# An audio tower with 64 experts: waits in place of a memset ahead of each indirect transfer

## The chip, the cores and the metric

The kernel runs on one core of a Trainium2 chip. The metric is the time of one execution on the device in microseconds (us). A core has five engines that work side by side, each with an instruction queue of its own: PE (TensorE, matmuls), DVE (VectorE), ACT (ScalarE), POOL (GpSimd) and SP (SyncE, which here only issues transfers). They are held together by semaphores: an instruction may wait for one to reach a count, and raise one when it is done.

## The reference

The input x is 128 series of 125 positions with 64 channels, float32. The convolution has a stride of two, so 128 x 63 = 8064 tokens are left. Three stages follow one another: the convolution with a norm over time and channels and a PReLU, a selective scan over 64 channels x 16 states, and a layer of 64 experts of which each token uses two. The change touches the third.

```python
    h = _L0_tok_ref(x, L0_tok_w, L0_tok_b, L0_tok_gamma, L0_tok_beta, L0_tok_alpha)
    h = h + _L0_attn_ref(_layernorm(h, axis=-1), L0_attn_A_log, L0_attn_D_param, L0_attn_scale, L0_attn_W_dt, L0_attn_b_dt, L0_attn_W_B, L0_attn_b_B, L0_attn_W_C, L0_attn_b_C)
    h = h + _L0_ffn_ref(_layernorm(h, axis=-1), L0_ffn_Wr, L0_ffn_br, L0_ffn_W1, L0_ffn_b1, L0_ffn_W2, L0_ffn_b2)
```

and the third of them:

```python
        logits = xf @ Wr + br
        topk_logits, topk_idx = jax.lax.top_k(logits, TOP_K)
        gates = jax.nn.softmax(topk_logits, axis=1)
        combine = jnp.zeros((T, E), xf.dtype).at[jnp.arange(T)[:, None], topk_idx].add(gates)
        out = jnp.zeros((T, W2.shape[-1]), xf.dtype)
        for e in range(E):
            h = jax.nn.relu(xf @ W1[e] + b1[e])
            y = h @ W2[e] + b2[e]
            out = out + combine[:, e:e + 1] * y
```

The kernel doesn't run all 64 experts over all tokens. It sorts the tokens by expert, runs each expert over its own rows, and takes the two results of a token back.

## The kernel before

All tokens lie on 128 partitions x L = 63 positions. After the convolution and the scan (the first 390 us or so) comes the expert layer, in these parts:

**Routing.** The positions are cut into three shares, SHARES = (0 to 16), (16 to 40), (40 to 63), and into eight groups of 8 positions (QG = 8): groups 0 and 1 are share 0, groups 2 to 4 share 1, groups 5 to 7 share 2. For each group PE transposes the normalised rows (transposes_of, L760) and makes the logits, ACT copies them out of PSUM (nT_copy, L1099), DVE finds the two best experts (choose) and writes a 0/1 table of them (L1503, which raises s_hot by one for each group). PE counts the tokens of each expert with matmuls on that table (counts_of, L775), DVE and ACT take the counts out (offsets_of, L1509), and DVE turns them into slot_i, for each token and choice the row of a sorted table in DRAM (slots_of, L1544, raising s_slot). DVE and PE do the routing of all three shares before they start on the experts.

**Scatter.** POOL writes each token's normalised row (64 floats) to its slot in sorted_rows[h], with an indirect transfer for each position and choice: 128 rows a transfer, 126 transfers in all (send, L613), share after share. Each raises s_disp[h].

**Experts.** They run in 80 steps: 24 for share 0, 28 for share 1, 28 for share 2. A step takes up to two pairs of tiles of 128 rows. Per step: PE transposes the rows (rows_T, L870); ACT copies them (xT_copy, L1151); PE makes the hidden layer (hidden, L881); ACT takes one half of the relu (relu_A, L1160) and DVE the other (relu_B, L1593); PE makes the outputs (outputs, L894, which waits for the y_copy of the step before); DVE copies them out of PSUM (y_copy, L1603, raising s_yb by one for each step); ACT stores them to expert_out[h] (store, which raises s_st). ACT starts a share's steps when all of that share's scatters have landed (s_disp[h]). SP loads the weights into a ring of 23 pairs and waits for s_yb before it writes over one.

**Gather.** POOL waits until all stores of a share are done (s_st, 4 semaphores) and then fetches each token's two result rows from expert_out[h] with indirect transfers into y1 and y2: 126 transfers in all (L634), 32, 48 and 46 for the shares. Each raises s_yl.

**Combine.** After the 80 steps DVE works through a block that builds the combine table (L1620, L1627), adds the bias product that PE makes of it, and then, group by group, multiplies y1 and y2 by the gates (gate_rows, L1635) and adds them to hg (L1637), waiting for s_yl; SP stores each finished group to out.

Ahead of each of POOL's 252 indirect transfers stands a memset: 128 x 128 zeros into a tile `beat` that nothing reads. It goes through ch.link, which makes the next instruction of POOL wait until the memset has ended (it raises POOL's own semaphore s_pool, and the transfer waits for it). All of this is code in a fixed order on each engine's queue; no scheduler moves it.

```python
                        ch.link(pool.memset(beat[:, :], 0.0))
                        pool.indirect_dma_start(
                            out=sorted_rows[h], out_offset=bass.IndirectOffsetOnAxis(ap=slot_i[:, c, l:l + 1], axis=0),
                            in_=xn[:, l, :], in_offset=None).then_inc(s_disp[h], 16)
```

In what follows transfers are counted d = 0 to 251 in the order of POOL's queue: d0 to 31, 32 to 79 and 80 to 125 are the scatters of the three shares, d126 to 157, 158 to 205 and 206 to 251 the gathers.

## Time and profile before

| | us |
|---|---|
| median of 3 runs (lowest, highest) | 925.29 (922.06 to 929.41) |
| the profiled execution: its time | 921.33 |
| its span, first to last instruction | 919.6 |
| PE busy | 555.3 (60%) |
| DVE busy | 568.8 (62%) |
| ACT busy | 332.5 (36%) |
| POOL busy | 654.9 (71%) |
| mean granted TensorE clock | 0.772 of full speed |

The profiled execution took 921.33 us, of which 1.7 us lie outside its span. All rows that follow are of this one execution; times in them count from the start of the span. "Idle before" is how long an engine stood still ahead of an instruction, with what ended it: another engine's line, a transfer, "issue" (nothing that the profile shows), or "remote" (the semaphore moved without an instruction in the profile that moved it at that time).

### The profile page before, as it was taken

The numbers are of one execution on the slowest core, as the hardware profiler recorded it, in microseconds if no ns is written. First come the engines' busy times: TensorE is split into PE (matmuls) and PEld (weight loads), VectorE is DVE, ScalarE is ACT, GpSimd is POOL, SyncE is SP. The second block draws the span as 40 slices with busy tenths as digits, with TensorE's granted clock in tenths as the row PEclk, the third lists the DMA queues.
The fourth block names the chain that finished last, engine by engine and source line by source line (L and its number), as shares of the span: only waits on it lengthen the run. The fifth ranks groups of instructions, "written<-read, shape, count | busy, mean of one in ns | idle before, by whom it ended". The sixth has DMA issues, their size and how long they took to land.

```text
span 919.6 us, 9334 instructions
## 1 busy us (share of the span) xinstructions
PE 555.3 (60%) x2514; PEld 372.0 (40%) x2520; DVE 568.8 (62%) x1180; ACT 332.5 (36%) x622; POOL 654.9 (71%) x645
## 2 busy tenths in 40 slices
PE   4653347575674575768556756577679765794230
PEld 4642012122221221244324545565568554683230
DVE  1697899999999999876464511132234211247964
ACT  2169756466466554342132111122224211241010
POOL 5894699999999999706848888763740387503884
PEclk9967576898798887775767667798799875797565
DMA  7999900000000000002600344467578844651012
GB/s 238 384 156 116 44 0 0 0 0 0 0 0 0 1 0 0 0 1 75 162 14 26 112 137 131 129 171 206 151 207 227 240 133 119 173 151 43 22 56 70
DMA packets 106607, 84.98 MB, mean 92 GB/s; under 512 B 30464, under 2 KB 90240, under 8 KB 106560
## 3 DMA queue, kind: packets, MB, share of 16 engines
q1 hardware_dynamic: 79312, 54.76, 27.4%
q10 hardware_dynamic: 19184, 21.40, 7.4%
q0 software_dynamic: 8064, 8.27, 3.4%
q8 instruction: 19, 0.31, 0.1%
q14 instruction: 28, 0.23, 0.1%
HBM read 57.22 MB, written 33.49 MB: 99 GB/s over the span
## 4 chain that ended last, share of the span: by engine, by line
PE 32%; POOL 30%; issue 16%; DVE 10%; another core or an unknown queue 4%; ACT 4%; SPq 1%; DMA 1%; POOLq 0%; ACTq 0%; DVEq 0%
PE ps L894 15%; POOL x_w L570 12%; POOL w_ring L563 11%; PE ps L881 6%; POOL xt L634 5%; PE ps L870 2%; PE ps L659 2%; PE ps L723 1%; PE ps L750 1%; POOL beat L633 1%; PE ps L808 1%; PE ps L745 1%; DVE lstat L1280 1%; DVE mi L1498 1%
## 5 line engine op out<-in xcount | busy, mean ns | idle before, releaser
L723 PE MATMUL ps<-x_w,ident 128*128 128x512 f32 x252 | 154.3, 771 | 102.0 <-POOL x_w L570 102.0
L563 POOL TENSOR_TENSOR w_ring<-xt,bc 128x2016 f32<-128x2016 f32 x32 | 144.7, 4524 | 13.4 <-DVE hh_ring L1409 7.3
L634 POOL DMA_INDIRECT xt<-expert_out,slot_i x126 | 123.6, 981 | 37.0 <-issue 21.9
L613 POOL DMA_INDIRECT sorted_rows<-xp,slot_i x126 | 123.0, 976 | 35.9 <-issue 18.4
L1409 DVE TENSOR_TENSOR_SCAN hh_ring<-ps,w_ring 128x1024 f32<-128x1024 f32 x64 | 145.7, 2277 | 0.1
L570 POOL TENSOR_TENSOR x_w<-hh_ring,bc 128x2016 f32<-128x2016 f32 (+1 forms) x32 | 142.4, 4456 | 2.3 <-PE ps L723 2.3
L723 PEld LDWEIGHTS ps<-x_w,ident 128*128 128x128 f32 x252 | 60.0, 249 | 199.0 <-POOL x_w L570 125.7
L633 POOL MEMSET beat<- 128x128 f32 x126 | 27.5, 218 | 106.3 <-DMA expert_out<-x_w 106.1
L1603 DVE COPY x_w<-ps 128x256 f32<-128x256 f32 x80 | 33.9, 424 | 109.2 <-PE ps L894 58.8
L1060 ACT ACTIVATE ps<-dt_t,a_exp 128x1024 f32<-128x1024 f32 x64 | 71.5, 1117 | 63.7 <-DVE hh_ring L1409 63.6
L1054 ACT ACTIVATE ps<-dt_t,a_exp 128x1024 f32<-128x1024 f32 x64 | 71.5, 1118 | 51.9 <-DVE w_ring L1388 51.9
L894 PE MATMUL ps<-dt_t,x_w 128*128 128x192 f32 x280 | 66.8, 389 | 30.6 <-issue 23.1
L1151 ACT ACTIVATE x_w<-ps 128x256 f32<-128x256 f32 x80 | 30.7, 384 | 149.3 <-PE ps L870 60.5
L1388 DVE TENSOR_TENSOR w_ring<-ps,w_ring 128x1008 f32<-128x1008 f32 x64 | 76.7, 1198 | 3.4 <-ACT ps L1054 3.4
L1403 DVE SCALAR_TENSOR_TENSOR w_ring<-ps,w_ring 128x1008 f32<-128x1008 f32 x64 | 75.5, 1180 | 0.0
L894 PEld LDWEIGHTS ps<-dt_t,x_w 128*128 128x128 f32 x280 | 54.5, 224 | 36.5 <-issue 34.1
L894 PE MATMUL ps<-x_w 128*128 128x192 f32 x224 | 53.1, 386 | 17.4 <-issue 16.7
L1593 DVE TENSOR_SCALAR x_w<-ps,dt_t 128x128 f32<-128x128 f32 x70 | 21.5, 345 | 54.0 <-remote 30.9
L894 PEld LDWEIGHTS ps<-x_w 128*128 128x128 f32 x224 | 43.5, 223 | 21.8 <-issue 19.9
L612 POOL MEMSET beat<- 128x128 f32 x126 | 27.5, 219 | 31.6 <-DVE slot_i L1544 31.5
L894 PE MATMUL ps<-bc,x_w 128*128 128x192 f32 x136 | 33.0, 391 | 25.6 <-issue 24.1
L870 PE MATMUL ps<-ident,x_w 128*128 128x128 f32 x160 | 37.3, 326 | 11.4 <-DMA x_w<-sorted_rows 11.1
(211 smaller groups left out, 956.1 us busy)
## 6 DMA issues: line engine op xcount, KB each, us to landing
dt_t<-packed SPq DMA_DIRECT2D x140, 96.5 KB
x_w<-packed SPq DMA_DIRECT2D x112, 96.5 KB
x_w<-sorted_rows ACTq DMA_DIRECT2D x40, 256.0 KB
expert_out<-x_w ACTq DMA_DIRECT2D x80, 128.0 KB
sorted_rows<-pad_rows SPq DMA_DIRECT2D x2, 3584.0 KB, 24.2
bc<-packed SPq DMA_DIRECT2D x68, 96.5 KB
packed<-in_L_ffn_W SPq DMA_DIRECT2D x3, 2048.0 KB, 39.4
x_w<-in_x SPq DMA_DIRECT2D x7, 448.0 KB, 9.8
```

The source lines that it names most:

```text
L563: pool.tensor_tensor(w_buf(k, 2), up3[:, bass.ds(c * DC, DC), 1:S].unsqueeze(1).broadcast_to([P, 2, DC, L]), vec_of(k, 2), ALU.mult).then_ ...
L570: pool.tensor_tensor(hc_buf(k, n), h_buf(k, n), vec_of(N + k, n), ALU.mult).then_inc(s_hcp, n)
L613: pool.indirect_dma_start(out=sorted_rows[h], out_offset=bass.IndirectOffsetOnAxis(ap=slot_i[:, c, l:l + 1], axis=0), in_=xn[:, l, :], in_ ...
L634: pool.indirect_dma_start(out=y[:, l, :], out_offset=None, in_=expert_out[h], in_offset=bass.IndirectOffsetOnAxis(ap=slot_i[:, c, l:l + 1] ...
L723: ins = pe.matmul(ps[:, i, :], ident[:, :], src[:, i * BANK:(i + 1) * BANK], start=(k < 0), stop=(k == (N - 2 if last else N - 1)), skip_g ...
L870: last = pe.transpose(ps[:, i % 2, j * P:(j + 1) * P], rows_in[:, u % RING, in_share(n) % UNIT, :], ident[:, :])
L894: last = pe.matmul(ps[:, 6 + j, t * OUT:(t + 1) * OUT], hT_e[:, i % 2, t, j, :], w_of(n)[:, t, 0:OUT], start=True, stop=True)
L1054: act.activation(banks(6, 2), d, ACT.Tanh, scale=a_exp[:, 2, k:k + 1]).then_inc(s_th, 1)
L1060: act.activation(banks(2 + 2 * (k % 2), 2), d, ACT.Exp, scale=a_exp[:, 1, k:k + 1]).then_inc(s_dA, 1)
L1388: dve.tensor_tensor(wv, body(banks(6, 2)), wv, ALU.mult).then_inc(s_g, 1)
L1403: dve.scalar_tensor_tensor(out=wv, in0=body(dA), scalar=1.0, in1=wv, op0=ALU.add, op1=ALU.mult).then_inc(s_b, 1)
L1409: dve.tensor_tensor_scan(hh_ring[:, k % 4, :], dA, w_ring[:, k % 4, :], 0.0, ALU.mult, ALU.add).then_inc(s_h, 1)
```

## The change

The tile `beat` and the 252 memsets are gone, and with them the wait of each transfer for s_pool. In their place stands keep_pace(d), which for most d does nothing. For six scatters it waits for s_hot (d18 until three groups' tables are made, d21 four, d25 five, d38 six, d41 seven, d44 eight). From d64 to d208 it waits ahead of every eighth transfer for s_yb, until so many steps' y_copy are done: 4, 8, 12, 16, 20, 25, 29, 33, 37, 41, 46, 50, 54, 58, 62, 66, 71, 75 and 79, that is about 4.2 steps for each eight transfers. Transfers 44 to 63, and 209 to 251, have no wait of this kind.

```diff
@@ -70,6 +70,13 @@
 OUT = 3 * C
 CQ = -(-L // 8)
 IDS = 32
+
+
+FIRST_STEP = 44
+LAG = 12
+EVERY = 8
+GROUP_AT = {18: 3, 21: 4, 25: 5, 38: 6, 41: 7, 44: 8}
+STEP_AT = {d: (d - FIRST_STEP - LAG) * STEP0[-1] // 153 for d in range(FIRST_STEP + LAG + EVERY, FIRST_STEP + LAG + 154, EVERY)}
 
 
 def slab(n):
@@ -189,7 +196,6 @@
         tile_e = sb("tile_e", [P, len(SHARES)])
         te = sb("te", [1, len(SHARES) * P], I32)
         b2w = sb("b2w", [P, P])
-        beat = sb("beat", [P, 128])
 
         uT = xt[0:C + 1, 0:3 * GL * P].rearrange("p (k n) -> p k n", k=3)
         dt = dt_t[:, :]
@@ -605,11 +611,18 @@
 
             pool.wait_ge(s_padw, 16 * len(SHARES))
 
+            def keep_pace(d):
+
+                if d in GROUP_AT:
+                    pool.wait_ge(s_hot, GROUP_AT[d])
+                if d in STEP_AT:
+                    pool.wait_ge(s_yb, STEP_AT[d])
+
             def send(h, g):
 
                 for c in range(2):
                     for l in range(span_of(g).start, span_of(g).stop):
-                        ch.link(pool.memset(beat[:, :], 0.0))
+                        keep_pace(2 * span_of(g).start + c * (span_of(g).stop - span_of(g).start) + l - span_of(g).start)
                         pool.indirect_dma_start(
                             out=sorted_rows[h], out_offset=bass.IndirectOffsetOnAxis(ap=slot_i[:, c, l:l + 1], axis=0),
                             in_=xn[:, l, :], in_offset=None).then_inc(s_disp[h], 16)
@@ -630,7 +643,7 @@
                         continue
                     for c, y in enumerate((y1, y2)):
                         for l in range(a, z):
-                            ch.link(pool.memset(beat[:, :], 0.0))
+                            keep_pace(2 * L + 2 * a + c * (z - a) + l - a)
                             pool.indirect_dma_start(
                                 out=y[:, l, :], out_offset=None, in_=expert_out[h],
                                 in_offset=bass.IndirectOffsetOnAxis(ap=slot_i[:, c, l:l + 1], axis=0)
```

The scatter's start on POOL's queue. Before (L600 and L601 are the layer norm of a group, numbers of buffers left out):

```order
L600 TENSOR_TENSOR xp<-hg,lsm 128x192 [waits s_nmr]
L601 TENSOR_TENSOR xp<-xp,lsm 128x192 [waits s_pool]
L612 MEMSET beat 128x128 [waits s_slot,s_padw]
L613 DMA sorted_rows<-xp,slot_i 12288x64 [waits s_pool]
L612 MEMSET beat 128x128
L613 DMA sorted_rows<-xp,slot_i 12288x64 [waits s_pool]
```

The same place now:

```order
L626 DMA sorted_rows0<-xp1,slot_i 12288x64 [waits s_slot,s_padw]
L626 DMA sorted_rows0<-xp1,slot_i 12288x64 x15
L626 DMA sorted_rows0<-xp1,slot_i 12288x64 [waits s_slot]
L626 DMA sorted_rows0<-xp1,slot_i 12288x64
L626 DMA sorted_rows0<-xp1,slot_i 12288x64 [waits s_hot]
L626 DMA sorted_rows0<-xp1,slot_i 12288x64 x2
L626 DMA sorted_rows0<-xp1,slot_i 12288x64 [waits s_hot]
L626 DMA sorted_rows0<-xp1,slot_i 12288x64 x3
```

Each transfer had a memset ahead and a wait for it; now 16 stand one behind the other, and then come waits for the slots and for the routing's tables.

The end of share 1's scatters and the start of share 2's, which lie beside the experts' steps. Before:

```order
L612 MEMSET beat 128x128
L613 DMA sorted_rows1<-xp1,slot_i 14336x64 [waits s_pool]
L612 MEMSET beat 128x128 [waits s_slot]
L613 DMA sorted_rows2<-xp1,slot_i 14336x64 [waits s_pool]
L612 MEMSET beat 128x128
L613 DMA sorted_rows2<-xp1,slot_i 14336x64 [waits s_pool]
L612 MEMSET beat 128x128
```

Now:

```order
L626 DMA sorted_rows1<-xp1,slot_i 14336x64 x19
L626 DMA sorted_rows1<-xp1,slot_i 14336x64 [waits s_yb]
L626 DMA sorted_rows1<-xp1,slot_i 14336x64 x7
L626 DMA sorted_rows1<-xp1,slot_i 14336x64 [waits s_yb]
L626 DMA sorted_rows1<-xp1,slot_i 14336x64 x7
L626 DMA sorted_rows2<-xp1,slot_i 14336x64 [waits s_yb,s_slot]
```

The memsets are gone, 20 transfers (the one that waits for s_hot and the x19) stand without a wait between them, and from there on each eighth transfer waits for the experts' steps.

The last scatters and the first gathers, before:

```order
L612 MEMSET beat 128x128
L613 DMA sorted_rows2<-xp1,slot_i 14336x64 [waits s_pool]
L633 MEMSET beat 128x128 [waits s_st2,s_st3,s_st1,s_st0]
L634 DMA xt<-expert_out0,slot_i 128x64 [waits s_pool]
L633 MEMSET beat 128x128
L634 DMA xt<-expert_out0,slot_i 128x64 [waits s_pool]
```

Now:

```order
L626 DMA sorted_rows2<-xp1,slot_i 14336x64 [waits s_yb]
L626 DMA sorted_rows2<-xp1,slot_i 14336x64 x5
L647 DMA xt<-expert_out0,slot_i 128x64 [waits s_st2,s_st3,s_st1,s_st0]
L647 DMA xt<-expert_out0,slot_i 128x64
L647 DMA xt<-expert_out0,slot_i 128x64 [waits s_yb]
L647 DMA xt<-expert_out0,slot_i 128x64 x7
L647 DMA xt<-expert_out0,slot_i 128x64 [waits s_yb]
L647 DMA xt<-expert_out0,slot_i 128x64 x7
```

The four waits for the stores have moved from the memset to the first gather, and the s_yb waits go on in groups of eight through the gathers of shares 0 and 1.

## Rows read from the trace of the kernel before

**Rows 1.** The page, parts 1 and 4: busy time of each engine; chain by line.
```profile
PE 555.3 (60%) x2514; PEld 372.0 (40%) x2520; DVE 568.8 (62%) x1180; ACT 332.5 (36%) x622; POOL 654.9 (71%) x645
...
PE ps L894 15%; POOL x_w L570 12%; POOL w_ring L563 11%; PE ps L881 6%; POOL xt L634 5%; PE ps L870 2%; PE ps L659 2%; PE ps L723 1%; PE ps L750 1%; POOL beat L633 1%; PE ps L808 1%; PE ps L745 1%; DVE lstat L1280 1%; DVE mi L1498 1%
```

**Rows 2.** The page, part 5: costliest groups (count | busy us, mean ns | idle before).
```profile
L634 POOL DMA_INDIRECT xt<-expert_out,slot_i x126 | 123.6, 981 | 37.0 <-issue 21.9
L613 POOL DMA_INDIRECT sorted_rows<-xp,slot_i x126 | 123.0, 976 | 35.9 <-issue 18.4
...
L633 POOL MEMSET beat<- 128x128 f32 x126 | 27.5, 218 | 106.3 <-DMA expert_out<-x_w 106.1
```

**Rows 3.** Timeline of POOL: start us, us, engine, line, operation [idle before].
```profile
552.55 0.97 POOL L613 DMA_INDIRECT sorted_rows<-xp,slot_i  x1 [0.28 <-POOL beat L612]
553.53 0.22 POOL L612 MEMSET beat<- 128x128 f32 x1
554.02 0.97 POOL L613 DMA_INDIRECT sorted_rows<-xp,slot_i  x1 [0.28 <-issue]
```

**Rows 4.** Line L1603 (one instruction a step) in four windows: count, duration, first and last start.
```profile
L1603 DVE COPY x_w<-ps x18: 410/424/425, 523.7 to 612.4; 128x256 f32<-128x256 f32 x18
...
L1603 DVE COPY x_w<-ps x10: 415/424/425, 640.3 to 681.2; 128x256 f32<-128x256 f32 x10
...
L1603 DVE COPY x_w<-ps x12: 410/425/425, 735.7 to 798.1; 128x256 f32<-128x256 f32 x12
...
L1603 DVE COPY x_w<-ps x19: 415/425/426, 681.2 to 723.4; 128x256 f32<-128x256 f32 x19
```

**Rows 5.** Groups by line on POOL in the first three of these windows.
```profile
L613 POOL DMA_INDIRECT sorted_rows<-xp,slot_i x63 | 61.4, 974 | 18.1 <-issue 11.2 <-POOL beat L612 6.9
...
L634 POOL DMA_INDIRECT xt<-expert_out,slot_i x27 | 25.9, 958 | 8.1 <-issue 7.3 <-POOL beat L633 0.8
...
L634 POOL DMA_INDIRECT xt<-expert_out,slot_i x43 | 41.2, 958 | 12.4 <-issue 11.1 <-POOL beat L633 1.4
```

**Rows 6.** Busy time by window: window, length, PE, PEld, DVE, ACT, POOL, PE clock, DMA share, GB/s.
```profile
524.00:616.00 92.00, 59.77 (x332) 50.57 (x330) 18.21 (x54) 18.09 (x54) 74.04 (x125) 0.76 0.50 144
681.00:724.00 43.00, 40.79 (x304) 35.15 (x302) 18.56 (x55) 16.92 (x52) 0.00 (x0) 1.00 0.81 228
735.00:797.00 62.00, 39.01 (x203) 33.42 (x202) 10.77 (x31) 10.49 (x31) 49.56 (x85) 0.72 0.51 139
```

**Rows 7.** Waits (total, times, longest us): 527 to 616, 681 to 724, POOL's in the whole.
```profile
DVE x_w L1593 <- remote: 39.4, 13, 4.6
...
DVE x_w L1603 <- PE ps L894: 18.3, 18, 1.8
...
POOL beat L633 <- DMA expert_out<-x_w: 106.1, 3, 46.4
```

**Rows 8.** Timeline in the steps: a PE product and the DVE line that reads it.
```profile
548.24 1.23 PE L881 MATMUL ps<-x_w,dt_t 64*128 64x128 f32 x8
...
555.76 0.61 DVE L1593 TENSOR_SCALAR x_w<-ps,dt_t 128x128 f32<-128x128 f32 x2 [3.88 <-remote]
```

**Rows 9.** Timeline of the routing's stage: waits for PE's work, and the first step.
```profile
445.18 0.60 ACT L1099 ACTIVATE xt<-ps 128x512 f32<-128x512 f32 x1 [7.06 <-remote]
...
492.21 0.60 ACT L1099 ACTIVATE xt<-ps 128x512 f32<-128x512 f32 x1 [4.71 <-remote]
...
498.17 1.09 DVE L1503 TENSOR_TENSOR hh_ring<-ps,top 128x896 bf16<-128x896 f32 x1
...
503.48 0.23 DVE L1509 TENSOR_SCALAR small_i<-ps 128x64 int32<-128x64 f32 x1 [4.04 <-remote]
...
516.63 1.12 PE L870 MATMUL ps<-ident,x_w 128*128 128x128 f32 x4 [0.37 <-issue]
```

**Rows 10.** Timeline of DVE at the end, gate_rows of the last positions.
```profile
907.28 0.36 DVE L1635 TENSOR_TENSOR xt<-xt,top 128x192 f32<-128x192 f32 x1 [1.30 <-DMA xt<-expert_out,slot_i]
...
911.80 0.36 DVE L1635 TENSOR_TENSOR xt<-xt,gate 128x192 f32<-128x192 f32 x1 [3.77 <-DMA xt<-expert_out,slot_i]
```

## The prediction

> **What bounds the kernel now.** I read the page's busy times first, then the chain, then the steps by window, then single waits.
>
> POOL is busy for 71% of the span and PE for 60% [rows 1], so neither fills it. The chain of what ended last runs through PE's L894 (15%), through POOL's two scan lines, which the change leaves alone, and only for 5% through the gathers. POOL isn't the engine that everybody waits for in the expert layer: it waits itself, three times and for 106.1 us in all, for the experts' stores [rows 7]. So 252 memsets less on POOL are worth little by themselves. The question is what POOL's transfers do to the steps.
>
> That is seen in line L1603, of which each step has one [rows 4]. With no transfer on POOL, 18 intervals between steps took 723.4 − 681.2 = 42.2 us, 2.34 us a step. In the three windows in which POOL transfers, 17 + 9 + 11 = 37 intervals took 88.7 + 40.9 + 62.4 = 192.0 us, 5.19 us a step. These steps do the same work. At the undisturbed pace 37 would take 86.6 us, so 105.4 us are lost. In 192.0 us POOL issues 131 transfers at 1.47 us each (start to start, 552.55 to 554.02 [rows 3]; the rows that count them in nearly the same windows say 63 + 27 + 43 = 133 [rows 5]). That is a loss of 0.80 us for each transfer, or 0.55 of the time in which POOL transfers, and 133 × 0.80 = 106 us over the layer.
>
> It isn't the DMA engines' load: from 681 to 724, the fast window, their share is 0.81 and 228 GB/s are moved, against 0.50 and 144 GB/s from 524 to 616 [rows 6]. Nor is it arithmetic: PE is busy for 60 of those 92 us. It is waiting. PE's L881 ended at 548.24 + 1.23 = 549.47, its reader on DVE began at 555.76 and is put down to "remote" after 3.88 us of idle time [rows 8]; such waits of that one line come to 39.4 us in 13 times, where in the fast window each step's y_copy waits about 1 us, for PE itself [rows 7]. So PE's finished work becomes known to ACT and DVE late while POOL transfers. That the hold depends on POOL I read from the windows; how it comes about the trace doesn't say.
>
> The Trainium skill ("Trainium Architecture — The Big Picture", section "What this means for kernel authors") says that engines are independent processors and that one doesn't block another unless a semaphore stands between. By that rule only the tail (below) would change, 5 us. The rows on the steps speak against it here: no semaphore leads from POOL's transfers to PE's readers inside a step.
>
> **The change, part by part.** *The memsets.* A memset takes 0.22 us and the wait for it 0.28, the transfer 0.97 (recorded mean 0.981 and 0.976 [rows 2]); the memset begins where the transfer before ends, 552.55 + 0.97 = 553.52 [rows 3]. Without both, transfers in a burst should follow at 0.97 us in place of 1.47. The trace has no two transfers back to back, so the bounds of this price are 0.97 and 1.47; I take 0.97, since memset starts follow the recorded ends to 0.01 us.
>
> *The tail.* The last 46 gathers wait for all stores, so 46 × 0.50 = 23 us come off POOL there. But DVE, which reads them, is busy with its own block meanwhile. It waits for gathers only twice at the very end, 1.30 and 3.77 us [rows 10]. So the tail gives 5 us, and the rest of the 23 disappears under DVE. If the faster transfers slowed DVE instead, it would be nothing: bounds 0 and −5. I take **−5**.
>
> *The steps.* After the change d64 to d205, 142 transfers, lie beside the steps, each eight of them released by 4.2 steps. Eight at 0.97 are 7.8 us and 4.2 undisturbed steps 9.8, so POOL seldom runs ahead of or far behind its table, and the waits alone cost nothing: what stands behind them on POOL's queue are scatters that the next share needs only when the present one is done (d120, the last wait ahead of share 2's rows, asks for 33 of the 52 steps before it), and gathers that only the combine reads. What 142 transfers cost the steps has three prices:
> - *Each transfer lets as much pass as before.* 37 steps passed in 131 transfers, 0.28 of a step or 0.66 us' worth. Loss 0.97 − 0.66 = 0.31, × 142 = 44 us, against 106: **−62**.
> - *The same share of the time is lost.* 0.55 × 0.97 = 0.53, × 142 = 75 us: **−31**.
> - *Nothing passes while transfers follow one another*: 0.97 × 142 = 138 us: **+32**.
>
> The row nearest to this question is 548.24 to 555.76 [rows 8]: the hold lasted over several transfers and the gaps between them, so the gap with the memset isn't a gate through which everything goes at once. That speaks for one of the first two; I take the middle, −31.
>
> *The routing.* ACT and DVE waited 7.06, 4.71 and 4.04 us for PE's finished work between 419 and 516 [rows 9]. The s_hot waits keep POOL quiet in the blocks of the first two: d21 is held until group 3's table, d25 until group 4's. Gain 12 us. But d44 to d63 are released together once group 7's table stands, at 499.3 [rows 9], and run 20 × 0.97 = 19.4 us beside the last part of the routing, 17.3 us long up to the first step at 516.63. In it a hold of 4.04 stood before; I count it twice, +4, which leaves **−8**. At best −12; at worst everything in it waits until the burst ends, 19.4 − 4.0 = +15.
>
> *Sum*: −5 − 31 − 8 = −44 against the execution's own 921.3, so 877. Its median is 4.0 above this one (925.3), so 881 is the forecast, between 846 (−5 − 62 − 12) and 967 (0 + 32 + 15, −5 for the tail, +4).
>
> **The rivals.** *Held for whole bursts, slower.* The wait for the memset may be what now lets PE's word through: 0.28 us in each 1.47 in which POOL's queue stands. Eight transfers back to back have none, twenty of them neither. Then 0.97 × 142 = 138 and the +15 of the routing: 921.3 + 32 + 15 − 5 + 4 = 967; with PE idle for long, its clock, 0.76 and 0.72 of full speed beside transfers against 1.00 from 681 on [rows 6], starts each undisturbed stretch low too, a few us more. It decides from a loss of 106 / 142 = 0.75 us for a transfer on, that is when under 0.22 us' worth of step passes in 0.97 where 0.66 passed in 1.47. For it: some gap must matter, and the change removes all but one in eight. Against it: the hold outlasts several of these gaps. Chance 0.32.
>
> *The transfers don't get closer.* If a transfer needs its 1.47 whatever stands ahead, each loses 0.80 still, 142 × 0.80 = 114, +8; the tail gives nothing, and the routing's −8 stays: about 921 to 929. The trace's regular spacing allows it; the memset's start at the recorded end of the transfer speaks against. On this the Trainium skill ("Perfetto Trace Analysis", section "GPSIMD Engine Instruction") says that a GpSimd span is unreliable and start-to-start spacing is to be used; by it the known price is 1.47 with a memset, and the 0.97 is not known. Chance 0.07.
>
> *The hold has nothing to do with POOL's queue.* Then only the tail's 5 us come, 920. The windows in rows 4 and 6 speak against. Chance 0.04.
>
> **How the numbers follow.** Faster, by the first or second price: 0.57, between 846 and 910. The two rivals near 920 to 929: 0.11. Held for bursts: 0.32, from 935 to 975. The likeliest is the second price, 881; its own range is 846 to 910. For 8 in 10 I reach from 850 to 960, leaving out 0.05 below and some 0.15 above. One per cent, about what a measurement of this kernel tells from no change, is 916 to 934.5.
>
> **What the changed profile would show.** Right: starts of L626 and L647 about 1.0 us apart in groups of eight, with POOL waiting for DVE's y_copy between groups; y_copy at about 3.4 us a step on average over the steps with transfers, since 4.2 undisturbed steps and eight times 0.53 make 14 us; waits put down to "remote" of L1593 and L1603 smaller in sum; the last L1635 without a wait for a transfer; L870's first step before 516. The slower rival: inside each burst of eight no y_copy at all, 7.8 us long, and 17.5 us for each group of 4.2 steps, ACT and DVE waiting until the burst's end; a hole of up to 19 us after group 7's table. The spacing rival: starts 1.4 us apart with "issue" between. The forecast is wrong as a whole if y_copy's spacing inside a burst is not about 2.34 / 0.45 = 5.2 us, or if the routing's last part grows by more than 5 us.

## The result, and the profile after

The changed kernel takes 960.8 us (median of 4, 959.7 to 964.9; a fifth run took 955.0) where the kernel before takes 925.9 beside it: a ratio of 1.037, 95% interval 1.031 to 1.043. It is slower by 35 us; I had forecast 881. On other chips the same two kernels stood otherwise to each other, 1.076 on one and 0.967 on another, and that turned out to be part of the cause (experiments, below). In two experiments of round three one run each, of 1194.5 and 873.3 us, lay far above its fellows and is left out of the ratios.

The profiled execution of after took 964.9 us, span 963.1, against 921.3 and 919.6. Where the 43.5 us came in is seen from y_copy, which is L1616 now: the expert layer's lines stand 13 further down, so the hidden layer is L894 (it was L881), the outputs L907 (it was L894) and DVE's relu L1606 (it was L1593). All 80 y_copies, after and then before:

```profile
L1616 DVE COPY x_w<-ps x80: 410/424/426, 529.7 to 856.4; 128x256 f32<-128x256 f32 x80
```

```profile
L1603 DVE COPY x_w<-ps x80: 410/425/426, 523.7 to 837.7; 128x256 f32<-128x256 f32 x80
```

The first y_copy comes 6.0 us later than before, the stretch from first to last takes 326.7 us in place of 314.0 (+12.7), and from the last one to the end of the span it is 106.7 in place of 81.9 (+24.8). The sum is 43.5.

The costliest groups on POOL (page, part 5; they answer to [rows 2]):

```profile
L626 POOL DMA_INDIRECT sorted_rows<-xp,slot_i x126 | 122.0, 968 | 157.5 <-DVE x_w L1616 67.2
...
L647 POOL DMA_INDIRECT xt<-expert_out,slot_i x126 | 120.0, 952 | 122.1 <-DVE x_w L1616 77.0
```

A transfer is still recorded at 0.97 and 0.95 us. But this is how two follow one another without a memset (timeline of POOL; answers to [rows 3]):

```profile
540.06 0.97 POOL L626 DMA_INDIRECT sorted_rows<-xp,slot_i  x1 [0.30 <-issue]
541.33 0.97 POOL L626 DMA_INDIRECT sorted_rows<-xp,slot_i  x1 [0.30 <-issue]
```

Start to start they are 1.27 us apart, not 0.97: an idle time of 0.30, put down to "issue", stands where the wait for the memset stood. The removal saves 0.20 us a transfer, not 0.50.

One round of eight transfers, d72 to d79, and the y_copies in it (timeline of all engines; POOL's row of 555.06 and that of 572.17 are the first transfers of two rounds):

```profile
555.06 0.96 POOL L626 DMA_INDIRECT sorted_rows<-xp,slot_i  x1 [6.41 <-DVE x_w L1616]
556.73 0.42 DVE L1616 COPY x_w<-ps 128x256 f32<-128x256 f32 x1 [0.95 <-issue]
563.76 0.42 DVE L1616 COPY x_w<-ps 128x256 f32<-128x256 f32 x1 [3.79 <-remote]
564.33 2.90 PE L907 MATMUL ps<-bc,x_w 128*128 128x192 f32 x8 [4.48 <-DVE x_w L1616]
567.33 0.42 DVE L1616 COPY x_w<-ps 128x256 f32<-128x256 f32 x1
570.99 0.42 DVE L1616 COPY x_w<-ps 128x256 f32<-128x256 f32 x1 [1.52 <-PE ps L907]
572.17 0.97 POOL L626 DMA_INDIRECT sorted_rows<-xp,slot_i  x1 [7.25 <-DVE x_w L1616]
```

This round lasts 17.1 us (the one before it 16.3, the two after it 16.0 and 17.9), and 4.2 undisturbed steps would be 9.8. The first y_copy comes 2.4 us after the one before it, undisturbed; then nothing for 7.0 us, while the transfers run; then two steps 3.6 and 3.7 us apart, for PE comes out of the hole with matmuls of 2.90 us for eight in place of 1.57 (the granted clock from 564.3 to 567.3 is 0.50 of full speed, that is 1.2 GHz; from 555 to 563 it was 1.00). The pace of 2.4 us is back only with the y_copy of 573.35, in the next round. POOL waits for steps meanwhile, 77.0 and 67.2 us in sum (waits over the whole span):

```profile
POOL xt L647 <- DVE x_w L1616: 77.0, 10, 9.3
POOL sorted_rows L626 <- DVE x_w L1616: 67.2, 7, 19.3
DVE x_w L1616 <- remote: 60.0, 16, 5.2
DVE x_w L1606 <- remote: 49.9, 18, 11.4
```

The "remote" waits of these two lines are fewer but longer: 16 and 18 in number, up to 11.4 us, against 23 and 24, up to 4.6, in the kernel before over its span. In sum they are hardly less, 109.9 against 114.0 us.

The tail has something that the trace of the kernel before doesn't show in the same block. After the last y_copy DVE builds the combine table with 126 small instructions that wait for nobody (timeline of DVE, before and then after):

```profile
838.12 14.14 DVE L1620 TENSOR_SCALAR us_lg<-iota_e,top 128x64 f32<-128x64 f32 x63
852.26 14.11 DVE L1620 TENSOR_SCALAR hh_ring<-iota_e,top,gate 128x64 f32<-128x64 f32 x63
866.40 4.90 DVE L1627 TENSOR_TENSOR us_lg<-us_lg,hh_ring 128x512 f32<-128x512 f32 x8
```

```profile
856.78 14.33 DVE L1633 TENSOR_SCALAR us_lg<-iota_e,top 128x64 f32<-128x64 f32 x63
...
871.11 6.42 DVE L1633 TENSOR_SCALAR hh_ring<-iota_e,top,gate 128x64 f32<-128x64 f32 x28
877.76 0.31 DVE L1633 TENSOR_SCALAR hh_ring<-iota_e,top,gate 128x64 f32<-128x64 f32 x1 [0.23 <-issue]
...
889.69 0.31 DVE L1633 TENSOR_SCALAR hh_ring<-iota_e,top,gate 128x64 f32<-128x64 f32 x1 [1.09 <-issue]
...
918.39 0.31 DVE L1633 TENSOR_SCALAR hh_ring<-iota_e,top,gate 128x64 f32<-128x64 f32 x1 [1.09 <-issue]
924.01 1.29 DVE L1640 TENSOR_TENSOR us_lg<-us_lg,hh_ring 128x512 f32<-128x512 f32 x2 [5.31 <-remote]
```

The first 91 run at 0.23 us each, while POOL's last 46 gathers are already under way (from 859.3). Then, at 877.8, DVE all but stops: an instruction each 0.7 or 1.4 us, with up to 1.09 us idle before it, until the gathers end; and L1640, which only waits for DVE's own raises of s_dve, starts 5.31 us after the last of them had finished. The block takes 67.2 us up to L1640 where it took 28.3. Of these 39 us the tail gets 14.1 back, for the gathers are over by then and what follows takes 39.1 us to the end of the span in place of 53.2.

### The profile page after: what moved, and what is told of

Same layout as the page of the kernel before. It is cut to its first block, busy times and chain, and to the rows that moved or that the text cites. A ratio compares the mean times of both kernels' runs of the same rounds, so it can differ in the third digit from the quotient of the medians.

```text
span 963.1 us, 9083 instructions
## 1 busy us (share of the span) xinstructions
PE 547.3 (57%) x2514; PEld 369.8 (38%) x2520; DVE 571.5 (59%) x1180; ACT 332.3 (35%) x622; POOL 595.2 (62%) x393
## 4 chain that ended last, share of the span: by engine, by line
PE 29%; POOL 21%; DVE 19%; issue 18%; another core or an unknown queue 8%; ACT 3%; SPq 1%; DMA 1%; POOLq 0%; ACTq 0%; DVEq 0%
PE ps L907 13%; POOL x_w L576 12%; POOL w_ring L569 9%; PE ps L894 6%; PE ps L883 2%; PE ps L672 2%; DVE hh_ring L1633 2%; DVE us_lg L1633 1%; DVE mi L1511 1%; DVE x_w L1606 1%; DVE hg L1650 1%; DVE x_w L1616 1%; DVE xt L1648 1%; DMA x_w<-sorted_rows 1%
## 5 line engine op out<-in xcount | busy, mean ns | idle before, releaser
L626 POOL DMA_INDIRECT sorted_rows<-xp,slot_i x126 | 122.0, 968 | 157.5 <-DVE x_w L1616 67.2
L736 PE MATMUL ps<-x_w,ident 128*128 128x512 f32 x252 | 152.3, 762 | 102.4 <-POOL x_w L576 102.4
L647 POOL DMA_INDIRECT xt<-expert_out,slot_i x126 | 120.0, 952 | 122.1 <-DVE x_w L1616 77.0
L1616 DVE COPY x_w<-ps 128x256 f32<-128x256 f32 x80 | 33.9, 424 | 134.9 <-PE ps L907 61.4
L907 PE MATMUL ps<-dt_t,x_w 128*128 128x192 f32 x280 | 67.0, 389 | 38.6 <-DVE x_w L1616 21.0
L907 PE MATMUL ps<-x_w 128*128 128x192 f32 x224 | 55.5, 399 | 31.5 <-DVE x_w L1616 16.2
L907 PEld LDWEIGHTS ps<-dt_t,x_w 128*128 128x128 f32 x280 | 55.0, 226 | 44.1 <-issue 38.2
L907 PEld LDWEIGHTS ps<-x_w 128*128 128x128 f32 x224 | 45.4, 232 | 36.1 <-issue 22.4
L1606 DVE TENSOR_SCALAR x_w<-ps,x_w 128x128 f32<-128x128 f32 x56 | 17.3, 346 | 56.1 <-remote 33.5
L1606 DVE TENSOR_SCALAR x_w<-ps,dt_t 128x128 f32<-128x128 f32 x70 | 21.5, 345 | 44.8 <-PE ps L894 33.4
L907 PE MATMUL ps<-bc,x_w 128*128 128x192 f32 x136 | 34.8, 408 | 21.4 <-DVE x_w L1616 13.5
L941 PE MATMUL ps<-ident,us_lg 128*128 128x128 f32 x32 | 5.5, 310 | 68.6 <-DVE us_lg L1640 68.6
L883 PE MATMUL ps<-ident,x_w 128*128 128x128 f32 x160 | 36.8, 322 | 11.7 <-DMA x_w<-sorted_rows 11.4
## 6 DMA issues: line engine op xcount, KB each, us to landing
packed<-in_L_ffn_W SPq DMA_DIRECT2D x3, 2048.0 KB, 39.1
```

What stands on the lines that cost most here:

```text
L626: pool.indirect_dma_start(out=sorted_rows[h], out_offset=bass.IndirectOffsetOnAxis(ap=slot_i[:, c, l:l + 1], axis=0), in_=xn[:, l, :], in_ ...
L647: pool.indirect_dma_start(out=y[:, l, :], out_offset=None, in_=expert_out[h], in_offset=bass.IndirectOffsetOnAxis(ap=slot_i[:, c, l:l + 1] ...
L736: ins = pe.matmul(ps[:, i, :], ident[:, :], src[:, i * BANK:(i + 1) * BANK], start=(k < 0), stop=(k == (N - 2 if last else N - 1)), skip_g ...
L907: last = pe.matmul(ps[:, 6 + j, t * OUT:(t + 1) * OUT], hT_e[:, i % 2, t, j, :], w_of(n)[:, t, 0:OUT], start=True, stop=True)
```

## The experiments

**Round one, on the chip on which the kernel before takes 922 us.** The record names no chip for the pair above; I take it to be this one, since before took 925.9 there and 922.1 here. Two theories are held apart: G, that the missing pause between transfers costs, and W, that the waits and the bunching do. Four kernels stand beside the same before.

The memset put back beside the waits, ahead of scatters and gathers:

```diff
+        beat = sb("beat", [P, 128])
...
+                        ch.link(pool.memset(beat[:, :], 0.0))
                         pool.indirect_dma_start(
                             out=sorted_rows[h], out_offset=bass.IndirectOffsetOnAxis(ap=slot_i[:, c, l:l + 1], axis=0),
...
+                            ch.link(pool.memset(beat[:, :], 0.0))
                             pool.indirect_dma_start(
                                 out=y[:, l, :], out_offset=None, in_=expert_out[h],
```

> The changed kernel with the memset and its wait put back ahead of each transfer, so only the s_hot and s_yb waits are added to the kernel before. Theory G (the gap): what costs is the missing 0.2 us pause between transfers, 1.27 us from start to start in place of 1.47. Then the waits alone cost or give little: 915 to 932 us, DVE's combine block 28 us as before, 8 transfers taking 11.8 us. Theory W (the waits): bunching transfers in eights behind the steps is what costs, and the pause is nothing: 945 to 965 us.

Measured: 875.6 us, ratio 0.947 (0.941 to 0.954). That is 46 us under before, more than either theory gave. Its y_copies (one line of the kernel: count, durations, first and last start):

```profile
L1619 DVE COPY x_w<-ps x80: 410/424/426, 513.7 to 792.0; 128x256 f32<-128x256 f32 x80
```

and a wait over the span (total, times, longest):

```profile
DVE x_w L1609 <- remote: 56.2, 30, 2.5
```

Against before: first y_copy 10.0 us earlier, first to last 278.3 us in place of 314.0, tail unchanged at 81.8. So W falls with the wrong sign: between the traced executions the waits are worth −46 of span, the memset's removal beside them +89. The forecast hadn't priced the waits in the steps at all.

Neither memset nor waits:

```diff
-                        ch.link(pool.memset(beat[:, :], 0.0))
-                            ch.link(pool.memset(beat[:, :], 0.0))
```

> The kernel before without memset and without any wait in its place: transfers follow one another at 1.27 us. Theory G: every stretch with transfers costs more than before and no rest lets the backlog out, 955 to 990 us, DVE's combine block 55 to 65 us in place of 28. Theory W: no bunching, so the steps lose what they lost before for each transfer or less, 905 to 928 us.

Measured: 1043.7 us, ratio 1.132 (1.125 to 1.139), beyond what G gave. The waits in question come in few pieces now (waits over the span):

```profile
DVE x_w L1590 <- remote: 83.0, 7, 26.2
ACT xt L1096 <- remote: 48.1, 1, 48.1
```

One wait of 48.1 us in the routing, seven of up to 26.2 in the steps: with a share's transfers on end, and no rest among them, PE's work is held for whole stretches. The four kernels are a table: both 876, memset alone 922, waits alone 961, neither 1044. Taking the pause away costs 85 us with the waits and 122 without; adding the waits gains 46 with the pause and 83 without. Rest of either kind gains on this chip, and the change traded the larger for the smaller. How much of the waits' gain is s_hot's (in the routing) and how much s_yb's wasn't tried apart; of the stretches above, the one up to the first y_copy gained 10.0 us and the steps 35.7.

The memset back ahead of the last 46 gathers alone:

```diff
                             keep_pace(2 * L + 2 * a + c * (z - a) + l - a)
+                            if h == 2:
+                                ch.link(pool.memset(beat[:, :], 0.0))
```

> The changed kernel with the memset back ahead of the last 46 gathers only. Theory G: DVE's combine block (126 tensor_scalar) falls from 62 to 28 us, the kernel by about 25, to 931 to 941 us; the rest stays. Rival: DVE's block is slow because the faster gathers take memory or ports from it; the pitch is only 1.27 against 1.47, so it would get back at most the ratio of the two, a few us: 950 to 961.

Measured: 935.8 us, ratio 1.013 (1.006 to 1.020), 25 under the changed kernel, as G had it. DVE's block:

```profile
853.98 14.15 DVE L1636 TENSOR_SCALAR us_lg<-iota_e,top 128x64 f32<-128x64 f32 x63
868.12 14.09 DVE L1636 TENSOR_SCALAR hh_ring<-iota_e,top,gate 128x64 f32<-128x64 f32 x63
```

The tail takes 81.9 us again, as before. So the whole +24.8 of the tail hangs on 0.2 us between these 46 transfers. Next, what of DVE is held? Only the last instruction of each loop raises s_dve:

```diff
                 for l in range(L):
...
-                    last.then_inc(s_dve, 1)
-                ch.at = ch.at + L
+                last.then_inc(s_dve, 1)
+                ch.at = ch.at + 1
```

> The changed kernel, but of the 63 tensor_scalar of each of the two loops of the combine block only the last raises s_dve, in place of each. POOL's queue is untouched. Theory Q (what is held is the raising of semaphores, in a queue that fills up until the engine itself stops): the block takes 28 us again and the kernel 931 to 941 us. Rival P (DVE's own reading and writing is held by POOL's transfers, through a port or memory): the block stays at 55 to 62 us, the kernel at 955 to 965.

Measured: 956.7 us, ratio 1.039 (1.032 to 1.046): a miss for Q, and not quite what P said either.

(timeline of DVE)

```profile
865.97 7.55 DVE L1633 TENSOR_SCALAR hh_ring<-iota_e,top,gate 128x64 f32<-128x64 f32 x32
...
904.83 0.31 DVE L1633 TENSOR_SCALAR hh_ring<-iota_e,top,gate 128x64 f32<-128x64 f32 x1 [1.09 <-issue]
914.65 1.89 DVE L1640 TENSOR_TENSOR us_lg<-us_lg,hh_ring 128x512 f32<-128x512 f32 x3 [9.51 <-remote]
```

The block still comes to a crawl, after 95 instructions in place of 91, and one single raise is seen 9.5 us late. From its first instruction (851.64) to L1640 it takes 63.0 us, against 67.2. So it isn't a matter of how many semaphores are raised. That something waits in line for each instruction, and the raise behind it, would fit; it isn't shown.

**Round two, on another chip, on which before takes 884 us.** The ratios are to before on the same chip. The length of the pause first: the kernel with waits and memset (a_waits_beat), with the memset four times and one sixteenth as wide. The cuts of this round, but for the last, are against that kernel:

```diff
-        beat = sb("beat", [P, 128])
+        beat = sb("beat", [P, 512])
```

> Waits and memset, the memset four times as wide (128x512), so that the transfers are further apart, about 2.0 us in place of 1.47. If the length of the pause is what lets the held raises through (theory G), holds of PE's work nearly vanish; but POOL then takes 8 x 2.0 = 16 us for each 4.2 steps and the last 46 gathers 92 us in place of 67, so POOL becomes the bound: 885 to 925 us, with the sum of the waits put down to remote on L1609 well under half of the 56 us. If the hold is a fixed price for each transfer, those waits keep their sum and the kernel goes to 900 to 940.

Measured: 883.3 us, ratio 1.000 (0.998 to 1.003), just under the range for a pause whose length counts. Pitch (timeline of POOL) and 21 of share 0's 24 y_copies (one line in a window):

```profile
505.39 0.97 POOL L628 DMA_INDIRECT sorted_rows<-xp,slot_i  x1 [0.28 <-POOL beat L627]
506.36 0.54 POOL L627 MEMSET beat<- 128x512 f32 x1
507.18 0.98 POOL L628 DMA_INDIRECT sorted_rows<-xp,slot_i  x1 [0.28 <-POOL beat L627]
```

```profile
L1619 DVE COPY x_w<-ps x21: 423/425/426, 501.4 to 548.6; 128x256 f32<-128x256 f32 x21
```

At 1.79 us from start to start there isn't one "remote" wait in the steps; these run 2.36 us apart beside the transfers as if there were none. POOL is the bound instead: share 0's steps end at 550.8 and share 1's begin 20 us later, and the last y_copy comes 164 us before the end. The hold is no fixed price of a transfer; it fades with the distance between them.

```diff
-        beat = sb("beat", [P, 128])
+        beat = sb("beat", [P, 8])
```

> Waits and memset, the memset one sixteenth as wide (128x8), so that each transfer still waits for POOL's own memset but the pause is short: about 1.33 us from start to start. Theory G (the length of the pause decides): between the two kernels, 900 to 955 us, nearer to the one without memset. Theory S (what helps is that the transfer waits for the instruction before it to end, at whatever length): 865 to 880 us.

Measured: 931.7 us, ratio 1.054 (1.049 to 1.059), at a pitch of 1.38 us:

```profile
551.09 0.97 POOL L628 DMA_INDIRECT sorted_rows<-xp,slot_i  x1 [0.28 <-POOL beat L627]
552.47 0.97 POOL L628 DMA_INDIRECT sorted_rows<-xp,slot_i  x1 [0.28 <-POOL beat L627]
```

Theory S falls: that the transfer waits for a memset is little help, the distance is what counts. With the changed kernel on this chip (949.4 us at 1.27, below) three kernels with the same waits stand in order of their pitch: 949 at 1.27, 932 at 1.38, 883 at 1.79. DVE's block doesn't come to a crawl at 1.38: its 126 instructions take 28.4 us, nearly 26 of them beside the last gathers. Then the bursts:

```diff
-EVERY = 8
+EVERY = 4
```

> Waits and memset (128x128), with a wait for the steps ahead of each fourth transfer in place of each eighth. If a hold builds up over several transfers in a row and a rest empties it, bursts of four lose less than bursts of eight: 855 to 872 us. If the loss is a fixed share of the time with transfers, nothing changes: 872 to 880.

Measured: 855.0 us, ratio 0.969 (0.965 to 0.973), and on a later occasion on this chip, as p_every4_again below, 855.2. Since a_waits_beat ran on the first chip, this tells that waits at each fourth with the memset beat before here as well; four against eight isn't told by it. Last, the changed kernel with the combine table from fewer and larger instructions (the cut is against the changed kernel):

```diff
-                for l in range(L):
-                    last = dve.tensor_scalar(comb[k][:, l, :], iota_e[:, :], top[:, 2 + k, l:l + 1], gates[k][:, l:l + 1],
-                                             ALU.is_equal, ALU.mult)
+                for q in range(CQ):
+                    v = span_of(q)
+                    shape = [P, v.stop - v.start, E]
+                    dve.tensor_tensor(comb[k][:, v, :], iota_e[:, :].unsqueeze(1).broadcast_to(shape),
+                                      top[:, 2 + k, v].unsqueeze(2).broadcast_to(shape), ALU.is_equal).then_inc(s_dve, 1)
...
+                    dve.tensor_tensor(comb[k][:, v, :], comb[k][:, v, :],
+                                      gates[k][:, v].unsqueeze(2).broadcast_to(shape), ALU.mult).then_inc(s_dve, 1)
```

> The changed kernel, with the combine table built eight positions at a time: 32 tensor_tensor of 128x512 in place of 126 tensor_scalar of 128x64, 22 us of work in place of 28. Theory N (each instruction of an engine sends something that has to get through beside the transfers, raise or none): 36 instructions in some 22 us are few enough, the block takes 22 to 28 us and the kernel 925 to 937. Theory P (DVE's own reads and writes are held by the transfers): the same bytes and more are moved, the block stays above 45 us and the kernel above 945.

Measured: 949.2 us, ratio 1.075 (1.071 to 1.079), no gain over the changed kernel on this chip (949.4, below).

The timeline of DVE:

```profile
848.36 4.82 DVE L1635 TENSOR_TENSOR us_lg<-iota_e,top 128x512 f32<-128x512 f32 x8
853.21 5.00 DVE L1642 TENSOR_TENSOR us_lg<-us_lg,top 128x512 f32<-128x512 f32 x8
...
868.15 5.06 DVE L1648 TENSOR_TENSOR us_lg<-us_lg,hh_ring 128x512 f32<-128x512 f32 x8
879.20 0.69 DVE L1664 TENSOR_TENSOR hg<-ps,hg 128x512 f32<-128x512 f32 x1 [5.99 <-issue]
907.20 0.69 DVE L1664 TENSOR_TENSOR hg<-ps,hg 128x512 f32<-128x512 f32 x1 [27.31 <-remote]
```

The block takes 24.9 us at full speed beside the same transfers. So P, as it was put, falls: DVE's reads and writes aren't slowed by the transfers as such, and in all these kernels the block starts at full speed. That it goes by the number of instructions is not shown by this. The last gathers began at 850.86 here and the block ended 22.3 us later; with small instructions on this chip DVE ran at full speed for 20.1 and 20.6 us beside them before its crawl (m_after_again and n_bare_again, below), on the first chip for 18.3 and 19.4 (the changed kernel and d_one_inc). A hold that sets in some 20 us after the gathers begin, whatever DVE does, is told from one that goes by the number of instructions only by these last 2 us, on one trace. The time is lost right behind. In the waits over the span:

```profile
ACT w_ring L1216 <- remote: 43.0, 3, 26.7
```

L1216 is ACT's copy of the transposed table, which PE needs for the bias product: ACT waits up to 26.7 us for transposes that PE has long made, and L1664, which needs the product, waits 27.3 us. With DVE early, this exchange between PE and ACT falls under the gathers, which it followed in the changed kernel. N was right on the block and wrong on the kernel.

**Round three, on a third chip: before takes 802 us.** That was the surprise of the study. Here are the trace of before and three kernels with memset beside it.

> The kernel before, unchanged, for its trace on this chip, because its median was 925 and 922 us on one chip and 884 on another. If the chips differ in how long the raises are held at a pitch of 1.47 us, then a chip on which it takes 884 shows a smaller sum of remote waits in the steps than the 39 us of the rows for L1593, and everything up to 416 us unchanged.

> Waits and memset again, beside the next two on one chip. Ratio to before 0.947 as on the first chip if the gain of the waits doesn't depend on the chip; if before loses less to holds on this chip, the waits have less to save: 0.96 to 0.98.

> Waits ahead of each fourth transfer, memset 128x128, beside the eighth. Theory B (a hold builds up over some transfers in a row, a rest empties it): 1 to 2.5% faster than waits at each eighth on the same chip. Theory C (a fixed price for each transfer): the same time within 0.5%.

> Waits at each fourth, and the memset 128x256 ahead of the first 206 transfers (about 1.58 us from start to start), 128x128 ahead of the last 46. At 1.79 us there were no remote waits at all in the steps. If the holds fade out between 1.47 and 1.79, POOL's own pace bounds the steps: 206 x 1.58 + some 20 of waits, then 82 us of tail: 840 to 850, that is 0.5 to 2% faster than each fourth with 128x128. If they fade only beyond 1.6, the slower pace costs: 858 to 875.

Measured: before 802.1 (the traced execution 801.7); waits and memset 801.8 (ratio 1.000, 0.999 to 1.001); each fourth 801.7 (0.999, 0.997 to 1.000); each fourth with 128x256 at a pitch of 1.58, 824.8 (1.027, 1.025 to 1.030). The expectation for the last took this for a chip with holds. The trace of before here, y_copies:

```profile
L1603 DVE COPY x_w<-ps x80: 424/425/426, 498.8 to 705.3; 128x256 f32<-128x256 f32 x80
```

and the end of DVE (timeline):

```profile
719.79 14.29 DVE L1620 TENSOR_SCALAR hh_ring<-iota_e,top,gate 128x64 f32<-128x64 f32 x63
...
792.20 0.36 DVE L1635 TENSOR_TENSOR xt<-xt,gate 128x192 f32<-128x192 f32 x1 [3.52 <-DMA xt<-expert_out,slot_i]
```

There is no "remote" wait on L1593 or L1603 at all, with the same transfers at the same 1.47 us. From the first y_copy to the last the same kernel takes 314.0 us on the first chip and 206.5 here, so I put 107.5 us there down to the holds, near the 106 of the prediction, and nothing here. With nothing held, POOL bounds the tail: DVE waits for gathers five times, up to 4.9 us, and a longer pause only costs.

**Round four, on the second chip again**, and **round five, on a fourth**, on which before takes 801.7:

> The changed kernel again, on another chip. Theory T (a threshold: the transfers and what the engines send share a way of limited rate, and the chips differ in it): where before takes 802 us and shows no holds at 1.47 us, 1.27 us may still be under the limit, then 785 to 800, or over it, then 830 to 960 with remote waits in the steps. Where before takes 922, 955 to 965. Rival: the change costs 35 us on any chip by its own waits: before + 30 to 40 everywhere, and no remote waits where before has none.

> No memset and no waits, again. Theory T: on a chip under its limit at 1.27 us, 778 to 795 (POOL gains 0.2 us x 160 transfers at the share ends and 5 to 9 us in the last 46 gathers); over it, 100 us and more above before.

> The kernel before for its trace on this chip. Theory T: the sum of remote waits on L1593 and L1603 grows with this chip's time for before: none at 802 us, some 60 at 922.

> Waits at each fourth with the memset 128x128. Theory T: where before is held (880 or more) 3 to 7% faster than it; where before isn't held, the same within 0.5%.

Measured beside before at 882.7: the changed kernel 949.4 (ratio 1.076, 1.072 to 1.079), the bare one 1039.7 (1.178, 1.174 to 1.181), each fourth with memset 855.2 (0.969, 0.966 to 0.973). The two kernels at 1.27 us take nearly what they took on the first chip; only the one at 1.47 us is 40 us faster here. So these two chips differ near that pitch, and at 1.27 both lose much. Of o_before_trace I had expected that the remote waits of L1593 and L1603 in sum follow the chip's time; they didn't (waits over the span):

```profile
DVE x_w L1593 <- remote: 76.3, 36, 3.8
DVE x_w L1603 <- remote: 36.1, 27, 3.1
```

On the first chip L1593's were 70.8 us in 24 waits and L1603's 43.2 in 23. The sums are 112.4 here and 114.0 there, though this chip is 40 us faster; here the waits are more in number and shorter.

> Waits at each eighth and the memset 128x128, beside the changed kernel on one chip. Theory G (the pause decides) with theory T (the chip's limit): where before takes 922 it takes 875, where before takes 883 some 865, where before takes 802 it takes 802.

> The changed kernel on the same chip. Theory G with T: 949 to 961 where before takes 883 to 922, so 80 to 90 us above the run with the memset beside it; where before takes 802, 785 to 800 if 1.27 us is under that chip's limit, else 830 or more with remote waits in the steps.

Measured on the fourth chip: waits and memset 801.8 (1.000, 0.999 to 1.002), the changed kernel **775.5 (0.967, 0.966 to 0.969)**. Here the change is 26 us faster, as T had it and below its range. The trace of r_after_third, y_copies:

```profile
L1616 DVE COPY x_w<-ps x80: 423/425/426, 494.1 to 700.8; 128x256 f32<-128x256 f32 x80
```

and the timeline of DVE after them:

```profile
715.58 14.40 DVE L1633 TENSOR_SCALAR hh_ring<-iota_e,top,gate 128x64 f32<-128x64 f32 x63
...
767.23 0.36 DVE L1650 TENSOR_TENSOR hg<-hg,xt 128x192 f32<-128x192 f32 x1
```

No remote wait in the steps, DVE's block in 28.7 us beside gathers that began at 1.26, last operation at 767.6 without a wait for a transfer. Against i_before, on the third chip, the last y_copy comes 4.5 us earlier and the tail takes 73.0 us in place of 94.7; against q_waits_beat_third, on this chip, it comes 1.2 us later and the tail takes 73.0 in place of 99.1. The rival that the change costs 35 us by itself on any chip is gone.

## Why the prediction was wrong

**What bounds the kernel** held up: the loss lay in steps beside transfers, PE's finished work came late, and it was POOL's transfers that did it. The reading that it isn't the load of the DMA engines is borne out: in r_after_third, where nothing is held, their mean share is 0.86 from 501 to 700.

```profile
501.00:700.00 199.00, 185.08 (x1354) 158.87 (x1353) 77.97 (x226) 75.40 (x224) 136.10 (x142) 0.96 0.86 252
```

**The price of the memset.** I took 0.97 for the pitch without it, because the memset starts where the recorded transfer ends. It is 1.27: 0.30 us of "issue" remain. The bounds held it, my choice didn't; all savings of POOL's time were 2.5 times too large (0.50 in place of 0.20 us). With 1.27 my own price for the steps, 0.55 of the time, would have been 0.70 us a transfer, 99 us, and its gain 7 us in place of 31.

**The steps (−31; measured +12.7).** This is the step that failed, and the pitch makes 24 of its 44 us; the rest is the rule by which I carried the loss over. I weighed three prices, by transfer, by share of time and by burst, and took the share of time (0.55 × 0.97 = 0.53 us a transfer). Measured over the four rounds from 538.79 to 606.05, 16.8 us each, it is (16.8 − 9.8) / 8 = 0.88 us in 1.27, a share of 0.69, and 142 × 0.88 = 125 us in place of 106: +19, of which +12.7 came (the other rounds weren't taken apart). All three prices assumed that the hold follows from the number of transfers or their time alone. The runs show it doesn't: it is nothing at 1.79 us on the second chip, nothing at 1.47 on two chips, 0.80 a transfer at 1.47 on the first, and there 0.88 at 1.27 with eights and rests between, on top of an engine that nearly stops in the tail. The cleanest pair has the same waits: from the first y_copy to the last it is 278.3 us at 1.47 (a_waits_beat) and 326.7 at 1.27, where a chip without holds takes 206.5. So with 0.20 us less between transfers the loss grew from 72 to 120 us, by two thirds, while the pitch shrank by a seventh. A way of limited rate that the transfers come near would act so, but that is a reading and not shown.

**The waits** I had costed at nothing beyond letting POOL rest in the routing. With the memset they gain 35.7 us in the steps, on the first chip; on the two chips without holds they gain nothing.

**The routing (−8; measured +6.0).** The quiet blocks did bring the first step forward, 516.6 to 513.7 (L883). But from there to the first y_copy, beside d44 to d63 in a row, it took 16.0 us in place of 7.1, with one "remote" wait of 11.4 us ahead of the first relu. With the memset (a_waits_beat) the first y_copy comes 10.0 us earlier than before, so −8 was right for the waits. The +15 that I had set for the worst case was near the +9 that this burst cost.

**The tail (−5; measured +24.8).** No rival had this: that DVE, which waits for no one there, could itself be stopped. I had written "if the faster transfers slowed DVE instead, it would be nothing" and bounded the loss at zero, without a row for it. In the trace of before the same block runs at full speed beside gathers at 1.47 us, and no transfers there stand closer, so nothing in it bounded the loss.

**The signs that I had named.** I called the forecast wrong as a whole if y_copy's spacing inside a burst wasn't about 5.2 us, or if the routing's last part grew by more than 5. It was 7.0 us in the round shown, and the part grew by 8.9. The sign "remote waits smaller in sum" came true, 109.9 against 114.0, in a kernel that is slower: it told nothing here.

**The rival that held for whole bursts** (967, chance 0.32) named the right sign, and its total lies 6 us from the median. It got there with a pitch that was too short, a loss in the steps that was too large (+32), and a tail that had the wrong sign, so that its total is near by luck. Inside a burst of eight one or two y_copies still come, not none. **The rival of the transfers that don't get closer** was closer on the pitch, 1.27 of 1.47, than my own choice of 0.97. The sentence of the Trainium skill ("Perfetto Trace Analysis", section "GPSIMD Engine Instruction") on start-to-start spacing agrees with these rows: the recorded 0.97 us leaves out 0.30 us of the 1.27 from start to start. Its other one ("Trainium Architecture — The Big Picture", section "What this means for kernel authors"), that engines don't block one another unless a semaphore stands between, agrees with the traces of two chips and not with the other two: DVE's crawl in the tail, an instruction in 1.4 us where it was one in 0.23, had no semaphore ahead of it.

**The chip** wasn't in the prediction at all. A forecast of 25 us faster would have been right on the fourth chip, though mainly for the tail (−21.7 against the third chip's before) and not for the holds.

**What stays open.** What is held, and which way it shares with POOL's transfers, isn't shown, nor whether DVE's crawl goes by the number of its instructions or by the time since the gathers began. Every run, timed ones too, has a span and a granted clock on record, so the records of the trace itself may be part of what waits in line; no run without them is among these. Nor is it known why chips differ, or whether one chip keeps its kind for long: the second gave 884 and 883 us for before in two rounds, the third and the fourth were measured once each. Bursts of four against eight were not compared on one chip with holds.

## What to carry to other kernels

An instruction that writes what nobody reads may be a spacer: before removing it, look whether other engines' finished work arrives late ("remote" waits, ends long before the reader's start) while the queue it stands in is busy, and measure the spacing both ways once, shorter and longer, before trusting a proportional estimate. Take the time of such an instruction from start to start, with and without it, not from what is recorded for its neighbour. Rests can be bought by waiting for the partner's progress, and here waits and spacer together were 5% faster than before on one chip with holds, each fourth 3% faster on another, and neither cost anything on chips without. Where a kernel's time differs by more than its spread between chips, a gain shown on one of them is no gain yet.

## What the runs showed of the hardware that was not expected

- Indirect transfers on POOL follow one another at 1.27 us (scatter; 1.26 gather) with nothing between, recorded as 0.97 and 0.95.
- Beside them the finished work of PE is seen late on two of four chips: at 1.27 us by up to 11.4 us in the changed kernel, and by 48.1 us in one wait with no rests (b_bare); at 1.79 us (e_beat512, second chip) not at all.
- On the same two chips DVE, with no wait ahead of it, falls from one small instruction in 0.23 us to one in 0.7 or 1.4 us after 18 to 21 us beside gathers at 1.26 us. Its last raise is then seen 5.3 to 9.5 us after the instruction has ended. At 1.38 us (f_beat8) and at 1.47 the same block runs at full speed.
- The same kernel took 922, 884, 802 and 802 us on four chips; the changed one 961, 949 and 775 on the first, the second and the fourth. On the fourth nothing is held at 1.27 us.
